# One broadcast product in place of four on GpSimd, in the scan of a Mamba block

## The reference, cut to what matters

```
x = x + 0.5 * ffn(layernorm(x))
x = x + mamba(layernorm(x))
x = x + 0.5 * ffn(layernorm(x))
```

```
dA = exp(delta[t, d] * negA[d, n])
h[d, n] = dA * h[d, n] + (delta[t, d] * x[t, d]) * B[t, n]
y[t, d] = sum over n of h[d, n] * C[t, n]
```

## Time and profile before

| what | value |
|---|---|
| median of 3 runs | 4300.07 us (4299.65 to 4301.24) |
| the profiled execution | 4301.24 us, span of its instructions 4299.4 us |
| VectorE busy over the span | 2871.6 us (67%) |
| GpSimd busy over the span | 2229.8 us (52%) |
| TensorE busy over the span | 3426.8 us (80%) |
| ScalarE busy over the span | 1997.2 us (46%) |
| the scans, from first to last (851.4 to 3235.0 us) | 2383.6 us |

### The profile page before, as it was taken

One profiled execution on the slowest core, in us unless ns is written; L12 is line 12 of the kernel. 1 busy time (PEld: TensorE's weight loads), 2 busy tenths in 40 slices (PEclk: granted clock), 3 DMA queues, 4 the chain that ended last, 5 costly groups with the idle time before them and its releaser, 6 DMA issues. The chain is left out here.

```text
span 4299.4 us, 63429 instructions
## 1 busy us (share of the span) xinstructions
PE 3426.8 (80%) x19584; PEld 2808.4 (65%) x19584; DVE 2871.6 (67%) x4386; ACT 1997.2 (46%) x5220; POOL 2229.8 (52%) x2735
## 2 busy tenths in 40 slices
PE   7999999776676667667766766766654999999999
PEld 7999999555455545545544554555443888888888
DVE  4222222199999999999999999999994222222222
ACT  4333333265565556556656655655653232223222
POOL 0010010288888988888888888889890000000000
PEclk9999999887788778778877877887756999999999
DMA  3000000301110110111011011101103111011100
GB/s 101 20 29 20 20 29 15 119 21 54 64 58 20 59 57 23 54 64 58 19 59 56 23 54 64 57 19 53 58 8 127 55 59 59 36 52 59 58 34 35
DMA packets 127125, 207.24 MB, mean 48 GB/s; under 512 B 42257, under 2 KB 63761, under 8 KB 126737
## 3 DMA queue, kind: packets, MB, share of 16 engines
q1 hardware_dynamic: 126864, 204.35, 13.8%
HBM read 151.97 MB, written 52.35 MB: 48 GB/s over the span
## 5 line engine op out<-in xcount | busy, mean ns | idle before, releaser
L361 POOL TENSOR_TENSOR ring<-dx,bb 128x256 f32<-128x256 f32 x2048 | 1776.5, 902 | 2.4 <-DMA bb<-scratch_bc 2.4
L628 DVE TENSOR_TENSOR_SCAN ring<-da,state_in,ring 128x256 f32<-128x256 f32 x2048 | 1363.8, 724 | 29.3 <-POOL ring L361 29.2
L404 ACT ACTIVATE da<-delta,neg_a 128x256 f32<-128x256 f32 x2048 | 894.1, 468 | 966.8 <-DVE ring L628 963.9
L562 PE MATMUL yps<-ident,hc 128*128 128x128 f32 x4096 | 728.6, 335 | 714.5 <-DVE hc L636 706.8
L562 PEld LDWEIGHTS yps<-ident,hc 128*128 128x128 f32 x4096 | 586.0, 172 | 913.3 <-DVE hc L636 878.3
L636 DVE TENSOR_TENSOR hc<-ring,cc 128x512 f32<-128x512 f32 x1024 | 880.6, 898 | 0.0
L855 POOL TENSOR_SCALAR second_rstd<-second_mv 128x1 f32<-128x1 f32 x32 | 8.5, 264 | 712.0 <-DVE second_mv L1023 712.0
L931 PE MATMUL first_mm<-first_h1hi,first_w2hi 128*128 128x256 f32 x1024 | 289.9, 283 | 8.1 <-DVE first_h1lo L1002 7.6
L931 PE MATMUL second_mm<-second_h1hi,second_w2hi 128*128 128x256 f32 x1024 | 288.6, 282 | 1.8 <-DVE second_h1lo L1002 1.8
L931 PE MATMUL first_mm<-first_h1lo,first_w2hi 128*128 128x256 f32 x1024 | 289.2, 282 | 0.0
L931 PE MATMUL first_mm<-first_h1hi,first_w2lo 128*128 128x256 f32 x1024 | 289.1, 282 | 0.0
(11 more groups left out here) (147 smaller groups left out, 6713.6 us busy)
## 6 DMA issues: line engine op xcount, KB each, us to landing
bb<-scratch_bc SPq DMA_DIRECT2D x64, 512.0 KB, 7.4
cc<-scratch_bc SPq DMA_DIRECT2D x64, 512.0 KB, 8.2
scratch_z<-zt SPq DMA_DIRECT2D x64, 256.0 KB, 2.0
scratch_y<-yt SPq DMA_DIRECT2D x64, 256.0 KB, 2.2
second_z<-scratch_z SPq DMA_DIRECT2D x32, 512.0 KB, 4.5
second_y<-scratch_y SPq DMA_DIRECT2D x16, 1024.0 KB, 6.5
first_x<-in_x SPq DMA_DIRECT2D x16, 512.0 KB, 3.6
scratch_x<-first_o SPq DMA_DIRECT2D x16, 512.0 KB, 2.8
```

The lines of the kernel that those rows point to most:

```text
L361: pool.tensor_tensor(ring[:, g, n, :], dx[:, j % 2, :], bb[1 - par][:, g * GROUP + n, :], ALU.mult).then_inc(dbx_done, 1)
L404: act.activation(da_slot(n), delta[:, j % 2, :], ACT.Exp, scale=neg_a[:, j * NS + n:j * NS + n + 1]).then_inc(da_done, 1)
L562: last = pe.matmul(y[:, a, :], hc[:, g, n, a * P:(a + 1) * P], ident[:, :], is_transpose=True, start=False, stop=(g == NG - 1 and n == GRO ...
L628: dve.tensor_tensor_scan(h, da_slot(n), h, state_in[par][:, i:i + 1], ALU.mult, ALU.add).then_inc(scanned, 1)
```

## The change

GpSimd's four products of a group become one instruction over all four states. `dx` is given a stride-0 axis of length 4, so that the one 128x256 tile is read four times; `bb` and `ring` are taken as 128x4x256. It counts `dbx_done` up once for each group and no longer four times. The two waits on that semaphore follow: SyncE's wait before it loads new `bb` rows counts groups, and VectorE waits once ahead of the four scans of a group, for the whole group, where it waited ahead of each scan for its own product.

```diff
@@ SyncE, broadcast_bc
-                    wait(dbx_done, GROUP * used)
+                    wait(dbx_done, used)
@@ GpSimd, body
-                        for n in range(GROUP):
-                            pool.tensor_tensor(ring[:, g, n, :], dx[:, j % 2, :], bb[1 - par][:, g * GROUP + n, :],
-                                               ALU.mult).then_inc(dbx_done, 1)
+                        pool.tensor_tensor(ring[:, g, :, :],
+                                           dx[:, j % 2, :].rearrange("p (o t) -> p o t", o=1).to_broadcast([P, GROUP, T]),
+                                           bb[1 - par][:, g * GROUP:(g + 1) * GROUP, :], ALU.mult).then_inc(dbx_done, 1)
@@ VectorE, scan_group
+                after(dve, dbx_done, q + 1)
                 for n in range(g * GROUP, (g + 1) * GROUP):
                     i = j * NS + n
-                    after(dve, dbx_done, k * NS + n + 1)
                     if n % 2 == 0:
                         after(dve, da_done, k * NS + n + 2)
```

## The result

The changed kernel takes 4622.37 us (median of 4 runs, 4618.70 to 4623.31), the kernel before 4299.86 us beside it: ratio 1.075, 95% interval 1.0734 to 1.0765. It is slower by 322 us. The forecast was 4647 us, with its own range of 4570 to 4783.

What follows compares the result with a forecast made beforehand. Bound: VectorE's work plus time GpSimd keeps its two-input SBUF instructions out. 15 x 21.7 + 20 + 1.7 = +347 us on 4301.2 gives 4648, put at 4647; own range 4570 to 4783, 8-in-10 range 4400 to 4790.

Steps and rivals of the forecast that it cites:

- given up inside X: Rival: GpSimd gives up the port between the four rows of 256, so the time is 4300 us; chance 0.08.
- X: GpSimd's new 128x1024 product instruction, one per group in place of four, or its length, forecast at 2.36 us.
- general sharing of the port: Alternative to full blocking between VectorE and GpSimd: a finely shared port, giving the time of before.
- Length of X: GpSimd's merged product: fixed 0.12 us plus 4 x 0.56 gives 2.36 us, bounds 2.24 to 2.72.
- the sum: Whole-run total: 15 front bodies at +21.7 us, last body +20, start +1.7, together +347 us.
- Two of four per block: Scan stage: two merged products hide under scans, two hold up VectorE by 2.1 to 2.3 us each; block loses 4.2.
- the 1.7 for the start: First scan: VectorE waits for the whole group, X less one product, 1.7 us once.
- the walk: Step-by-step timeline of one four-step block of scans, `hc` and GpSimd products, giving a loss of 4.2 us.
- VectorE's two `hc` go together: Rival: between the two `hc`, VectorE wins the port and every X hides under scans: 4032 us; chance 0.05.
- Only one X per block: Rival: GpSimd finds its `ring` slot taken one step earlier, so one blocks instead of two: 4350 us; chance 0.06.
- Three block: Rival: front work or late `delta` puts a third long product behind an `hc`, +270 us: 4917; chance 0.05.
- Supply: The experiments' rival theory: VectorE loses time because a group's products come all at once or GpSimd's lead changes.

Runs made afterwards that it cites:

- e3: Changed kernel with `hc` multiplying by a constant PSUM tile instead of C in SBUF, and two front PSUM banks instead of three: 4155.27 us.
- e4: Changed kernel with GpSimd's product of step q waiting until `hc` of step q-2 is done, where it waited for step q-4: 4160.68 us.
- e9: Changed kernel with GpSimd's product of step q waiting until `hc` of step q-3 is done, where it waited for step q-4: 4365.70 us.
- e1: Kernel before, four products of 256 kept, with only the changed kernel's counting and waits, once per group: 4297.59 us.
- e6: Kernel before with `hc` multiplying by a constant PSUM tile instead of C in SBUF, and two front PSUM banks: 4020.55 us.

## Why the prediction was right

**What bounds.** VectorE's list plus the time in which GpSimd keeps it out: shown. The scan stretch took the whole loss, and 317.0 of its 319.1 us lie on the four kinds of VectorE instruction that can be kept out. e3 shows it from the other side: with one input in PSUM the same `hc` loses nothing.

**An instruction of GpSimd blocks to its end, however long.** The prediction had this from 512 elements. It holds for 1024 elements in four rows: single `hc` of 2.82 us beside a product of 2.78.

```profile
3438.67 2.78 POOL L360 TENSOR_TENSOR ring<-dx,bb 128x1024 f32<-128x1024 f32 x1
```

```profile
3439.17 2.82 DVE L636 TENSOR_TENSOR hc<-ring,cc 128x512 f32<-128x512 f32 x1
```

The rival "given up inside X" falls with that, as does the general sharing of the port. The page "SBUF — State Buffer" of the Trainium skill ("Who interferes with whom"), which was weighed in the prediction, says that the instruction that comes later is fully blocked. The trace agrees, for an instruction of 2.3 us.

**Length of X.** Forecast 2.36 us. In the changed kernel the one that started at 3436.37 was followed by the next at 3438.67: 2.30. The estimate worked out from the page "GPSIMD Engine Reference" of the Trainium skill (section 3.1) was 2.31 us, and the trace agrees with it. The forecast was 0.06 us too long, twice per block: 15 us over 128 blocks, about half of the 28 us by which the sum was too high.

```profile
3436.37 2.33 POOL L360 TENSOR_TENSOR ring<-dx,bb 128x1024 f32<-128x1024 f32 x1
```

**Two of four per block.** The last body shows it. A free step takes 2.58 + 1.19 us, so the bare body is 119.5, and the block shown above lost 2.14 and 1.89 us to two X: 7 such blocks make 147.7, and it measures 147.8. The forecast had 153.7 with 8 x 4.2. It had counted a block too many: behind the last block there is no `prepare`, so its products are made early and hold nothing up. A front body was forecast at 171.7 and is (2702.7 - 147.8) / 15 = 170.3 on average.

**The sum.** Forecast +347, measured +319 in the scan stretch: 21 of the difference from the 15 front bodies (1.4 each), 6 from the last, and the 1.7 for the start, which lies ahead of this stretch (the first scan starts at 852.5 us, before at 851.4).

**What was off in the picture.** In the walk a waiting X always gets in between the two `hc`. In the changed kernel there are blocks where it doesn't: the timelines of VectorE and GpSimd, one block later.

```profile
3432.92 1.27 DVE L636 TENSOR_TENSOR hc<-ring,cc 128x512 f32<-128x512 f32 x2
3434.11 2.67 DVE L628 TENSOR_TENSOR_SCAN ring<-da,state_in,ring 128x256 f32<-128x256 f32 x4
3436.69 5.30 DVE L636 TENSOR_TENSOR hc<-ring,cc 128x512 f32<-128x512 f32 x2
```

```profile
3432.94 3.46 POOL L360 TENSOR_TENSOR ring<-dx,bb 128x1024 f32<-128x1024 f32 x1
```

X starts at 3432.94, 0.02 us behind the first `hc`, and both `hc` go before it (1.19 us for the pair). It then runs under the scans, and the next two hold up both `hc` of the following step: 5.23 us for that pair. In the last body 3 of the 7 blocks with a loss go this way. The number of long instructions that find no scans to hide under is two again, and the loss is the same (5.23 - 1.19 = 4.04 us, against 2.14 + 1.89), so the sum held although this step of it did not hold in every block. That is luck in part: the walk didn't have this case.

**The rivals.** "VectorE's two `hc` go together" happens, as just shown, but gives nothing back, since the X that is put off meets the next `hc`. Its price, everything hidden, needs the start of every X to be tied to the scans: e4 does that and gains 462 us, though its 4161 stays above the rival's 4032. "Only one X per block" was priced at 4350; e9 makes that case by its wait and takes 4366. "Three block", at 4917, did not come: the last body has two in each of its 7 blocks. "Supply" was none of the prediction's rivals, and e1 and e4 exclude it.

## What to carry to other kernels

In this kernel, a GpSimd instruction that reads SBUF, beside a VectorE that is busy with instructions of two SBUF inputs, is priced by what it keeps out: merging short ones saves their fixed part on GpSimd (0.12 us each here, hidden) and raises the price of each collision from 0.5 to over 2 us. So ask what VectorE is doing when the long instruction starts. If there is a stretch that does not need the port and is longer than the instruction (here four scans, 2.58 us against 2.30), make it start there with one wait: that turned a loss of 322 us into a gain of 140.

## What the runs showed of the hardware that was not expected

- A two-input VectorE instruction of 128x512 (`hc`) takes 0.664 us with its second input in PSUM, beside short and long GpSimd products alike (e3, e6); with both in SBUF its mean is 0.898 us beside the short products and 1.113 beside the long ones.
- VectorE instructions with one SBUF tile as input can be held up too: in the changed kernel 30 clamps of 128x256 last 2.43 us on average, where the shortest takes 0.28. The statistics of 128x512 (line 596) keep a mean of 0.67 us in the kernel before and in the changed one, the scans 0.72.
- Who gets the port at a near tie is not settled. A GpSimd instruction that started 0.02 us behind an `hc` let two `hc` pass in one block (3432.92 and 3432.94), while one 0.01 us behind got in between them in another (3413.80 and 3413.81). In e4 a `delta` that started 0.11 us ahead of an `hc` (2937.51 and 2937.62) let both pass and lasted 1.97 us. No run was made to separate these.
- Bare GpSimd products of two inputs start 0.68, 1.24 and 2.30 us apart for 256, 512 and 1024 elements, no more than the 2.36 of a line through the first two, so the stride-0 axis costs nothing that can be seen. (The 512 is the addition of the feed-forward passes.)
